# A matmul behind a sigmoid on one core: h made twice by ScalarE, and other shares of t for GpSimd

## The chip, the core and the metric

The kernel runs on one core of one Trainium2 chip. The time is the device time of one execution, in microseconds (us). Before the change three executions took 314.30, 316.69 and 318.40 us, median 316.69. A further execution was recorded by the hardware profiler; all rows here come from it.

Engines are called by their short names: PE (TensorE), DVE (VectorE), ACT (ScalarE), Pool (GpSimd), and SP (SyncE), which issues nearly all transfers. PEld is PE's loading of weights.

## The reference

```python
# x (1024, 24, 1024), W1 (1024, 24), b1 (1024), W2 (1024, 1024), b2 (1024), all fp32
h = jax.nn.sigmoid(jnp.einsum('bts,st->bs', x, W1) + b1)
return h @ W2.T + b2
```

x is 100.7 MB. For each row b and column s the 24 values over t are weighted and summed, b1 is added, the sigmoid gives h (1024 x 1024), and one product with W2 follows.

## The kernel before

**Stages.** There are four stages, each 512 rows of x by 512 columns s: stage 0 is rows 0 to 511, columns 0 to 511; stage 1 the same rows, the other columns; stages 2 and 3 are the other rows. One t of a stage is one ring load, [128, 4, 512] fp32, 1.05 MB (four row tiles of 128). A stage has 24 t.

**Two ways for a t.** The first t of a stage (4 in stage 0, 6 in the others: third number of its row in `STAGES`) go to Pool. They are loaded as halves of two row tiles into `nat` (6 slots, 0.52 MB each); Pool multiplies each half by its weights (`weigh`, L589) and adds it to the running sum of its half (`add_sum`, L598). The other t are loaded into `ring` (5 slots). PE transposes each (`turn_unit`, L303) into one of 6 PSUM banks `xbank`: a unit is one column block c of 128 columns (c = 0 to 3) with its 2 or 4 row tiles. DVE multiplies the unit by the weight, which now is one value a partition, and adds it to `acc` (`add_unit`, L423; the first unit of a stage and c is written by L417). Pool's sum of a stage is transposed in the same way, once, as four "n" units (DVE L421); before the change they stand ahead of the units of t = 22.

**Parts.** In stages 2 and 3 the last t (6 and 10) are loaded and summed in two parts: first row tiles 0 and 1 of all of them, then row tiles 2 and 3 of all of them. A ring slot then holds two half loads. The rows of part 1 are finished early and their products can run while part 2 is read.

**h and the products.** When a column block's sum is done, ACT makes h from it (L535) and rounds it to `h_hi` (fp32r, L539). DVE makes `h_lo` = h - h_hi (`low_part`, L437; in the last stage's last rows DVE does the rounding too, L472 and L474). W2 is transposed and split in the same way during stage 0 (L332, L498, L430). An output tile [128, 512] is 4 column blocks times three products, h_hi w_hi, h_hi w_lo and h_lo w_hi (L375). The product steps of stage i are dealt out between the units of stage i+1 by `steps_due` and the table `STRETCHES`. Sums of stages 0 and 2 are kept in `y` by ACT (`keep_out`, L523), those of stages 1 and 3 are added to it by DVE (`add_out`, L453) and stored. In the last stage 36 steps of part 1's rows lie between the units of part 2, 12 (`REST`) behind the last unit, and then the 48 products of the last rows follow (L401).

**Order of the loads.** SP issues in one fixed order: the ring loads of a stage one after the other, and ahead of those whose index is in the stage's tuple `places` a `nat` load of this or the next stage. Each waits for its slot:

```python
if m >= NATS and parts[m - NATS][1] < pools[parts[m - NATS][0]] - 1:
    sp.wait_ge(nat_added, sums_made(m - NATS + 2))
elif m >= NATS:
    sp.wait_ge(unit_turned, sum_turned(parts[m - NATS][0], parts[m - NATS][2]))
```

The second branch (L263's wait) is for a slot that held a stage's finished sum: it is free when PE has turned the n units of its rows. A ring load (L269) waits until the last unit of the load five slots back is turned. Whatever SP waits for, the loads behind it wait too.

Of the kernel before, what the change touches and what calls it, by code (L numbers as in the profile page):

```python
# [32 lines left out]
def rec_kernel(nc, x, W1, b1, W2, b2, out):  # L33
# [94 lines left out]
    with ExitStack() as ctx:  # L128
# [156 lines left out]
        def _(pe):  # L285
# [196 lines left out]
        def _(act):  # L482
            act.dma_start(b1row[:, :], b1.rearrange("(c p) -> c p", p=P)).then_inc(b1_loaded, 16)
            for p in (0, 32):
                act.dma_start(h[p:p + 1, 0:OH, :], b2.rearrange("(a h n) -> a h n", a=1, n=BANK)).then_inc(b2_loaded, 16)
# [44 lines left out]
            def sigmoid(i, p):  # L530

                c, row, n = sums[i][p]
                rows = slice(row * P, (row + n) * P)
# [1 line left out]
                nc.scalar.activation(h[:, c, rows], acc[:, c, rows], ACT.Sigmoid,  # L535
                                     bias=b1col[:, bass.ds(STAGES[i][1] + c, 1)]).then_inc(h_ready, 1)
# [88 lines left out]
```

## Time and profile before

| what | us |
|---|---|
| median of three executions | 316.69 |
| profiled execution | 314.37 |
| its span on the core | 312.5 |
| DVE busy | 268.9 |
| PE busy | 265.0 |
| Pool busy | 196.6 |
| ACT busy | 53.6 |
| mean granted clock of PE | 0.95 |

Busy time of an engine is no bound by itself: PE and DVE feed each other through `xbank`, and both wait for loads. GB/s over time says where transfers are the pace, the queue's own waits say what held SP, and the chain of work that ended last says what ran at the end. The duration of one matmul in the rows overlaps the next, so rates are taken from a run of them (time over count). The same holds for DVE.

### The profile page before, as it was taken

How to read it: one execution, taken by the hardware profiler on the slowest of the kernel's cores; microseconds unless marked ns; L12 is line 12 of the kernel's file. 1: busy time of each engine (PE TensorE's matmuls, PEld its weight loads, DVE VectorE, ACT ScalarE, POOL GpSimd, SP SyncE). 2: the span in 40 equal slices, each digit the busy share in tenths (PEclk: the TensorE clock that was granted, in tenths of full speed). 3: DMA queues.
4: the chain of work that ended last, by engine and by line, in shares of the span. 5: the costliest groups of instructions: out<-in, count | busy, mean ns of one | idle time of the engine just before them, and what ended most of it. 6: DMA issues, size and time to landing. Idle time of an engine off the chain costs nothing.

```text
span 312.5 us, 4880 instructions
## 1 busy us (share of the span) xinstructions
PE 265.0 (85%) x1761; PEld 227.6 (73%) x1761; DVE 268.9 (86%) x452; ACT 53.6 (17%) x97; POOL 196.6 (63%) x89
## 2 busy tenths in 40 slices
PE   0948788857887799999968699997699999999995
PEld 0847688747865588888756588886488888788884
DVE  0719997929989998888999999999999999899961
ACT  4201222302262011011140000004032001050200
POOL 3119766635379888985679996967979399700000
PEclk9968977979999999999989999999579999999999
DMA  7999999999999999999999999999979999992122
GB/s 218 393 388 387 387 385 387 402 386 387 386 387 386 387 386 387 386 386 387 385 386 387 386 393 389 396 385 388 381 265 343 398 387 387 387 387 111 68 103 101
DMA packets 55164, 109.48 MB, mean 350 GB/s; under 512 B 3418, under 2 KB 3426, under 8 KB 55140
## 3 DMA queue, kind: packets, MB, share of 16 engines
q1 hardware_dynamic: 54544, 107.06, 93.3%
q10 hardware_dynamic: 596, 2.11, 1.7%
q8 instruction: 14, 0.23, 0.3%
q14 instruction: 10, 0.08, 0.1%
HBM read 104.97 MB, written 4.19 MB: 349 GB/s over the span
## 4 chain that ended last, share of the span: by engine, by line
PE 53%; DMA 17%; issue 13%; DVE 9%; ACT 3%; SPq 3%; DVEq 0%; ACTq 0%
PE xbank L303 27%; PE pbank L375 19%; DMA ring<-in_r_x 17%; DVE acc L423 7%; PE xbank L401 3%; SPq L263 2%; ACT h L535 2%; PE pbank L321 2%; ACT h_hi L539 1%; PE pbank L365 1%; PE pbank L332 1%; DVE acc L421 1%; DVE y L453 1%; DVE w_lo L430 1%; SPq L269 1%
## 5 line engine op out<-in xcount | busy, mean ns | idle before, releaser
L423 DVE SCALAR_TENSOR_TENSOR acc<-xbank,w,acc 128x512 f32<-128x512 f32 (+1 forms) x344 | 203.5, 643 | 22.8 <-PE xbank L303 21.4
L303 PE MATMUL xbank<-ident,ring 128*128 128x128 f32 x1184 | 186.4, 285 | 39.1 <-DMA ring<-in_r_x 27.5
L303 PEld LDWEIGHTS xbank<-ident,ring 128*128 128x128 f32 x1184 | 151.3, 147 | 70.9 <-DVE acc L423 24.4
L589 POOL TENSOR_TENSOR nat<-nat,w1all 128x1024 f32<-128x1024 f32 x44 | 106.1, 2413 | 67.3 <-DMA nat<-in_r_x 53.5
L598 POOL TENSOR_TENSOR nat<-nat 128x1024 f32<-128x1024 f32 x36 | 87.1, 2420 | 2.8
L375 PE MATMUL pbank<-w_hi,h_hi 128*128 128x512 f32 x112 | 52.9, 472 | 1.8 <-DVE y L453 1.8
L375 PE MATMUL pbank<-w_lo,h_hi 128*128 128x512 f32 x112 | 51.6, 461 | 0.0
L375 PE MATMUL pbank<-w_hi,h_lo 128*128 128x512 f32 x112 | 45.8, 453 | 0.0
L535 ACT ACTIVATE h<-acc,b1col 128x256 f32<-128x256 f32 (+2 forms) x28 | 14.5, 536 | 93.3 <-DVE acc L423 93.2
L437 DVE TENSOR_TENSOR h_lo<-h,h_hi 128x256 fp32r<-128x256 f32 (+1 forms) x20 | 26.3, 1314 | 0.0
L375 PEld LDWEIGHTS pbank<-w_hi,h_hi 128*128 128x128 f32 x112 | 22.0, 197 | 2.2 <-DVE y L453 2.0
L523 ACT COPY y<-pbank 128x512 f32<-128x512 f32 x16 | 9.4, 587 | 81.1 <-PE pbank L375 81.1
L375 PEld LDWEIGHTS pbank<-w_lo,h_hi 128*128 128x128 f32 x112 | 22.2, 198 | 0.2
L417 DVE TENSOR_SCALAR acc<-xbank,w 128x512 f32<-128x512 f32 x16 | 11.8, 748 | 11.7 <-PE xbank L303 9.3
L375 PEld LDWEIGHTS pbank<-w_hi,h_lo 128*128 128x128 f32 x112 | 19.5, 190 | 0.2
L498 ACT CAST w_hi<-pbank 128x512 fp32r<-128x512 f32 x16 | 9.4, 587 | 39.5 <-PE pbank L332 39.5
L332 PE MATMUL pbank<-ident,y 128*128 128x128 f32 x64 | 10.5, 289 | 0.9 <-DVE w_lo L430 0.9
L303 PE MATMUL xbank<-ident,nat 128*128 128x128 f32 x64 | 10.6, 291 | 0.5 <-DVE acc L423 0.5
L421 DVE TENSOR_TENSOR acc<-xbank,acc 128x256 f32<-128x256 f32 (+1 forms) x24 | 10.9, 501 | 0.0
L430 DVE TENSOR_TENSOR w_lo<-pbank,w_hi 128x512 fp32r<-128x512 f32 x16 | 10.9, 680 | 0.0
L493 ACT COPY w1all<-pbank 128x512 f32<-128x512 f32 x12 | 7.0, 587 | 18.1 <-PE pbank L321 18.1
L539 ACT CAST h_hi<-h 128x256 fp32r<-128x256 f32 (+1 forms) x20 | 9.8, 491 | 0.6
(31 smaller groups left out, 93.9 us busy)
## 6 DMA issues: line engine op xcount, KB each, us to landing
ring<-in_r_x SPq DMA_DIRECT2D x58, 1024.0 KB, 12.9
nat<-in_r_x SPq DMA_DIRECT2D x44, 512.0 KB, 12.8
ring<-in_r_x SPq DMA_DIRECT2D x32, 512.0 KB, 11.5
y<-in_L_rec_W SPq DMA_DIRECT2D x2, 2048.0 KB, 15.3
out_y<-y ACTq DMA_DIRECT2D x4, 512.0 KB, 7.3
out_y<-y SPq DMA_DIRECT2D x8, 256.0 KB, 2.0
w<-in_L_rec_W SPq DMA_DIRECT2D x1, 96.0 KB, 2.5
h<-in_L_rec_b ACTq DMA_DIRECT2D x2, 4.0 KB
```

What stands on the lines that cost most here:

```text
L303: mm = pe.transpose(xbank[u % XBANKS][:, a * P:(a + 1) * P], tile, ident[:, :])
L332: mm = pe.transpose(pbank[m % 2][:, j * P:(j + 1) * P], y[:, j, c * P:(c + 1) * P], ident[:, :])
L375: mm = pe.matmul(pbank[n % 2][:, :], a[:, c, rows], w[:, STAGES[i][1] + c, cols], start=r == 0, stop=r == per - 1)
L417: nc.vector.tensor_scalar(total, bank, weight, None, ALU.mult).then_inc(unit_added, 1)
L421: nc.vector.tensor_tensor(total, bank, total, ALU.add).then_inc(unit_added, 1)
L423: nc.vector.scalar_tensor_tensor(out=total, in0=bank, scalar=weight, in1=total, op0=ALU.mult, op1=ALU.add).then_inc(unit_added, 1)
L430: nc.vector.tensor_tensor(w_lo[:, c, cols], pbank[m % 2][:, :], w_hi[:, c, cols].bitcast(F32), ALU.subtract).then_inc(w_lo_ready, 1)
L437: nc.vector.tensor_tensor(h_lo[:, c, rows], h[:, c, rows], h_hi[:, c, rows].bitcast(F32), ALU.subtract).then_inc(h_lo_ready, 1)
L535: nc.scalar.activation(h[:, c, rows], acc[:, c, rows], ACT.Sigmoid, bias=b1col[:, bass.ds(STAGES[i][1] + c, 1)]).then_inc(h_ready, 1)
L539: nc.scalar.copy(h_hi[:, c, rows], h[:, c, rows]).then_inc(h_hi_ready, 1)
L589: nc.gpsimd.tensor_tensor(slot, slot, row, ALU.mult).then_inc(nat_weighed, 1)
L598: nc.gpsimd.tensor_tensor(slot, slot, nat[:, (m - 2) % NATS, :, :], ALU.add).then_inc(nat_added, 1)
```

## The change

ACT makes h twice for every piece: first the sigmoid rounded straight into `h_hi`, then the same sigmoid in fp32 into one PSUM bank, `hbank`, from which DVE subtracts `h_hi` to make `h_lo`. `h` in SBUF is gone. Since there is one bank, the second sigmoid waits until the low part before it is made. The bank comes from `xbank` (6 to 5). The low parts move forward in DVE's order: of a whole stage, they stand behind the first four units of the next one. In the last rows ACT rounds too, not DVE.

Pool gets 7 t in stages 1 to 3 (6 before), `nat` 7 slots; the table of places changes with it. The last stage has 8 t in two parts (10 before). The n units of a stage or part move from ahead of t = 22 to behind t = 23. The row of b2 uses the last `nat` slot before its first load, which waits for `b2_ready`.

```diff
-    (4, 0, 6, 6, (0, 2, 3, 5, 6, 8, 9, 11, 12, 14, 18, 20, 21, 23), "keep"),
-    (4, 4, 6, 10, (1, 3, 4, 6, 7, 9, 11, 13), "last"),
+    (4, 0, 7, 6, (0, 1, 3, 4, 5, 7, 8, 9, 10, 12, 14, 17, 19, 21), "keep"),
+    (4, 4, 7, 8, (0, 1, 2, 4, 5, 6, 8, 9, 11, 13), "last"),
...
-    NATS = 6
-    XBANKS = 6
+    NATS = 7
+    XBANKS = 5
...
         for t, row, n in loads[i]:
-            if t == T - 2:
+            order += [("x", t, c, row, n) for c in range(NC)]
+            if t == T - 1:
                 order += [("n", 0, c, row, n) for c in range(NC)]
-            order += [("x", t, c, row, n) for c in range(NC)]
...
-        h = sb("h", [P, NC, BANK])
...
+        hbank = ctx.enter_context(nc.psum_tensor("hbank", [P, BANK], F32))
...
+        def h_held(i, p):
+
+            return hbank[:, :sums[i][p][2] * P]
...
+                        if m == NATS - 1:
+
+                            sp.wait_ge(b2_ready, 1)
...
             def low_part(i, p):
+
                 c, row, n = sums[i][p]
                 rows = slice(row * P, (row + n) * P)
-                dve.wait_ge(h_hi_ready, first_sum[i] + p + 1)
-                nc.vector.tensor_tensor(h_lo[:, c, rows], h[:, c, rows], h_hi[:, c, rows].bitcast(F32),
+                dve.wait_ge(h_ready, first_sum[i] + p + 1)
+                nc.vector.tensor_tensor(h_lo[:, c, rows], h_held(i, p), h_hi[:, c, rows].bitcast(F32),
                                         ALU.subtract).then_inc(h_lo_ready, 1)
...
-                if splits[i]:
-                    lows.update({part_end(i) + NC + 2 * c: (i, c) for c in range(NC)})
-                if i < LAST:
-                    lows.update({first_unit[i + 1] + NC + 2 * c: (i, len(sums[i]) - NC + c) for c in range(NC)})
+                for p in range(len(sums[i]) if i < LAST else TAIL):
+                    c, row, _ = sums[i][p]
+                    if splits[i] and row == 0:
+                        u = part_end(i) + 1 + 2 * c
+                    else:
+                        u = first_unit[i + 1] + c
+                    lows.setdefault(u, []).append((i, p))
...
-                nc.vector.tensor_copy(h_hi[:, c, rows], h[:, c, rows]).then_inc(tail_hi, 1)
-                dve.wait_ge(tail_hi, p - TAIL + 1)
-                nc.vector.tensor_tensor(h_lo[:, c, rows], h[:, c, rows], h_hi[:, c, rows].bitcast(F32),
+                nc.vector.tensor_tensor(h_lo[:, c, rows], h_held(LAST, p), h_hi[:, c, rows].bitcast(F32),
                                         ALU.subtract).then_inc(tail_lo, 1)
...
                 act.wait_ge(unit_added, sum_end(i, p))
-                nc.scalar.activation(h[:, c, rows], acc[:, c, rows], ACT.Sigmoid,
-                                     bias=b1col[:, bass.ds(STAGES[i][1] + c, 1)]).then_inc(h_ready, 1)
-                if i < LAST or p < TAIL:
-                    act.wait_ge(h_ready, first_sum[i] + p + 1)
-                    nc.scalar.copy(h_hi[:, c, rows], h[:, c, rows]).then_inc(h_hi_ready, 1)
+                tail = i == LAST and p >= TAIL
+                nc.scalar.activation(h_hi[:, c, rows], acc[:, c, rows], ACT.Sigmoid,
+                                     bias=bias).then_inc(tail_hi if tail else h_hi_ready, 1)
+
+                g = first_sum[i] + p
+                if tail and p > TAIL:
+                    act.wait_ge(tail_lo, p - TAIL)
+                elif g > 0:
+                    act.wait_ge(h_lo_ready, g)
+                nc.scalar.activation(h_held(i, p), acc[:, c, rows], ACT.Sigmoid, bias=bias).then_inc(h_ready, 1)
```

SP's order at the passage from stage 0 to stage 1. `nat` waits either for Pool's additions (nat_added) or for PE's transposes (unit_turned). Before:

```order
L263 DMA nat<-in_r_x 128x2x512 [waits nat_added]
L269 DMA ring<-in_r_x 128x4x512 [waits unit_turned] x2
L263 DMA nat<-in_r_x 128x2x512 [waits nat_added]
L269 DMA ring<-in_r_x 128x4x512 [waits unit_turned] x2
L263 DMA nat<-in_r_x 128x2x512 [waits nat_added]
L269 DMA ring<-in_r_x 128x4x512 [waits unit_turned]
L263 DMA nat<-in_r_x 128x2x512 [waits unit_turned]
```

Before, the first pair of ring loads here is the last of stage 0 (t = 22 and 23), and three ring loads of stage 1 stand ahead of the `nat` load that waits for unit_turned. After:

```order
L271 DMA nat<-in_r_x 128x2x512 [waits nat_added]
L277 DMA ring<-in_r_x 128x4x512 [waits unit_turned] x2
L271 DMA nat<-in_r_x 128x2x512 [waits nat_added]
L277 DMA ring<-in_r_x 128x4x512 [waits unit_turned]
L271 DMA nat<-in_r_x 128x2x512 [waits unit_turned]
```

After it, the first pair is again t = 22 and 23 of stage 0; one ring load of stage 1 stands ahead of the `nat` load that waits for unit_turned.

PE's order at the end of stage 0, where `xbank<-ident,nat` are the n units, `pbank<-ident,y` the transposes of W2, and `xbank<-ident,ring` the x units. Before:

```order
L303 MATMUL xbank<-ident,nat 128x128 x8
L332 MATMUL pbank<-ident,y 128x128 x4
L303 MATMUL xbank<-ident,nat 128x128 x8
L303 MATMUL xbank<-ident,ring 128x128 x4
L332 MATMUL pbank<-ident,y 128x128 x4
L303 MATMUL xbank<-ident,ring 128x128 x12
L332 MATMUL pbank<-ident,y 128x128 x4
L303 MATMUL xbank<-ident,ring 128x128 x52
```

After:

```order
L340 MATMUL pbank<-ident,y 128x128 x4
L311 MATMUL xbank<-ident,ring 128x128 x12
L340 MATMUL pbank<-ident,y 128x128 x4
L311 MATMUL xbank<-ident,nat 128x128 x16
L311 MATMUL xbank<-ident,ring 128x128 x36
```

The 16 transposes of the n units have moved behind all x units of the stage.

DVE's order at the start of stage 1, behind the last sum of stage 0. Before:

```order
L417 TENSOR_SCALAR acc<-xbank,w 128x512 [waits h_ready,unit_turned] x4
L423 SCALAR_TENSOR_TENSOR acc<-xbank,w,acc 128x512 [waits unit_added,unit_turned]
L437 TENSOR_TENSOR h_lo<-h,h_hi 128x512 [waits h_hi_ready]
L423 SCALAR_TENSOR_TENSOR acc<-xbank,w,acc 128x512 [waits unit_added,unit_turned] x2
L437 TENSOR_TENSOR h_lo<-h,h_hi 128x512 [waits h_hi_ready]
```

After:

```order
L426 TENSOR_SCALAR acc<-xbank,w 128x512 [waits h_ready,unit_turned]
L447 TENSOR_TENSOR h_lo<-hbank,h_hi 128x512 [waits h_ready]
L426 TENSOR_SCALAR acc<-xbank,w 128x512 [waits h_ready,unit_turned]
L447 TENSOR_TENSOR h_lo<-hbank,h_hi 128x512 [waits h_ready]
L426 TENSOR_SCALAR acc<-xbank,w 128x512 [waits h_ready,unit_turned]
```

Each low part now stands directly behind the first unit of its column block, and both wait for the second sigmoid.

## Rows read from the trace of the kernel before

**Rows 1.** The page, parts 1 and 2: busy us by engine; GB/s in 40 slices.
```profile
PE 265.0 (85%) x1761; PEld 227.6 (73%) x1761; DVE 268.9 (86%) x452; ACT 53.6 (17%) x97; POOL 196.6 (63%) x89
...
GB/s 218 393 388 387 387 385 387 402 386 387 386 387 386 387 386 387 386 386 387 385 386 387 386 393 389 396 385 388 381 265 343 398 387 387 387 387 111 68 103 101
```

**Rows 2.** The page, parts 3 and 6: bytes; a DMA issue with its size and us to landing.
```profile
HBM read 104.97 MB, written 4.19 MB: 349 GB/s over the span
...
out_y<-y SPq DMA_DIRECT2D x8, 256.0 KB, 2.0
```

**Rows 3.** SP's own waits by line: us in total, times, longest.
```profile
SPq L263 <- PE xbank L303: 24.9, 6, 11.1
```

**Rows 4.** SP's timeline from 212 us: start us, us, engine line operation.
```profile
214.64 2.49 SPq L269 DMA_DIRECT2D ring<-in_r_x  x2
...
228.23 0.37 SPq L263 DMA_DIRECT2D nat<-in_r_x  x1
```

**Rows 5.** Windows, stage 2 to 3: busy us by engine, PE clock, DMA share, GB/s.
```profile
core 0: us, PE busy (x) PEld busy (x) DVE busy (x) ACT busy (x) POOL busy (x), PEclk, DMA share, GB/s
...
221.00:223.00 2.00, 1.78 (x6) 1.28 (x6) 2.00 (x3) 0.00 (x0) 1.99 (x1) 0.50 1.05 388
...
225.00:227.00 2.00, 1.47 (x8) 0.86 (x6) 2.00 (x5) 0.00 (x0) 2.00 (x2) 0.50 0.91 339
...
227.00:229.00 2.00, 2.00 (x9) 1.64 (x8) 2.00 (x6) 0.00 (x0) 1.92 (x2) 0.50 0.23 89
...
229.00:231.00 2.00, 2.00 (x13) 1.64 (x12) 1.55 (x5) 0.00 (x0) 1.44 (x1) 0.76 0.79 209
...
235.00:237.00 2.00, 2.00 (x16) 1.76 (x15) 1.85 (x4) 0.95 (x2) 2.00 (x1) 1.00 0.83 247
...
237.00:239.00 2.00, 2.00 (x17) 1.76 (x15) 2.00 (x4) 0.59 (x1) 2.00 (x2) 1.00 0.91 306
```

**Rows 6.** Groups by line and shape: count, busy us, mean ns, idle before and releaser.
```profile
L535 ACT ACTIVATE h<-acc,b1col 128x512 f32<-128x512 f32 x8 | 5.8, 719 | 8.4 <-DVE acc L423 8.4
...
L437 DVE TENSOR_TENSOR h_lo<-h,h_hi 128x512 fp32r<-128x512 f32 x8 | 13.3, 1665 | 0.0
...
L437 DVE TENSOR_TENSOR h_lo<-h,h_hi 128x256 fp32r<-128x256 f32 x12 | 13.0, 1079 | 0.0
...
L430 DVE TENSOR_TENSOR w_lo<-pbank,w_hi 128x512 fp32r<-128x512 f32 x16 | 10.9, 680 | 0.0
...
L589 POOL TENSOR_TENSOR nat<-nat,w1all 128x1024 f32<-128x1024 f32 x44 | 106.1, 2413 | 67.3 <-DMA nat<-in_r_x 53.5 <-ACT w1all L493 13.8
...
L598 POOL TENSOR_TENSOR nat<-nat 128x1024 f32<-128x1024 f32 x36 | 87.1, 2420 | 2.8
```

**Rows 7.** Timeline of PE at the start of stage 1: start us, us, [idle, releaser].
```profile
88.03 2.30 PE L303 MATMUL xbank<-ident,ring 128*128 128x128 f32 x16 [0.50 <-DMA ring<-in_r_x]
```

**Rows 8.** Timeline of DVE: a run of full units; a low part with Pool quiet.
```profile
106.07 11.30 DVE L423 SCALAR_TENSOR_TENSOR acc<-xbank,w,acc 128x512 f32<-128x512 f32 x17
...
278.26 0.41 DVE L437 TENSOR_TENSOR h_lo<-h,h_hi 128x256 fp32r<-128x256 f32 x1
```

**Rows 9.** Timeline of Pool and of ACT: one load awaited, the first sum of part 1.
```profile
215.63 2.35 POOL L589 TENSOR_TENSOR nat<-nat,w1all 128x1024 f32<-128x1024 f32 x1 [0.32 <-DMA nat<-in_r_x]
...
275.30 0.51 ACT L535 ACTIVATE h<-acc,b1col 128x256 f32<-128x256 f32 x1 [1.81 <-DVE acc L423]
```

**Rows 10.** The chain that ended last: start us, us, engine, tile, line, count.
```profile
146.07 3.07 PE xbank L303 x28
...
266.38 0.63 PE xbank L303 x4
...
295.50 2.99 PE pbank L375 x13
...
298.50 10.89 PE xbank L401 x48
...
309.41 0.69 DVE y L453
```

More of the change, by code:

```diff
@@ L21 @@
 STAGES = (
-    (0, 0, 4, 0, (2, 3, 5, 7, 9, 11, 13, 15, 17, 18), "keep"),
-    (0, 4, 6, 0, (0, 2, 3, 5, 6, 8, 9, 11, 12, 14, 15, 17), "last"),
-    (4, 0, 6, 6, (0, 2, 3, 5, 6, 8, 9, 11, 12, 14, 18, 20, 21, 23), "keep"),
-    (4, 4, 6, 10, (1, 3, 4, 6, 7, 9, 11, 13), "last"),
+    (0, 0, 4, 0, (2, 3, 5, 7, 9, 11, 12, 13, 15, 16, 17, 18), "keep"),
+    (0, 4, 7, 0, (0, 1, 3, 4, 5, 7, 8, 9, 11, 12, 13, 14, 15, 16), "last"),
+    (4, 0, 7, 6, (0, 1, 3, 4, 5, 7, 8, 9, 10, 12, 14, 17, 19, 21), "keep"),
+    (4, 4, 7, 8, (0, 1, 2, 4, 5, 6, 8, 9, 11, 13), "last"),
 )
-CUT = 2
 NC = 4
@@ L41, in rec_kernel @@
     RING = 5
-    NATS = 6
-    XBANKS = 6
+    NATS = 7
+    XBANKS = 5
     REST = 12
+    CUT = JT // 2
     assert (B, T, S, O) == (2 * BANK, 24, 1024, 1024)
@@ L348, in product_step @@
                     n, r = (k - 2 * high) // NC, high + (k - 2 * high) % NC
-                first = n == 0
                 n += OH * row
@@ L368, in product_step @@
                     c, a, w = (r - bias) // 2, h_hi, (w_hi, w_lo)[(r - bias) % 2]
-                    if first:
+                    if n % (OH * CUT) == 0:
                         pe.wait_ge(h_hi_ready, first_sum[i] + sum_of(i, c, j) + 1)
@@ L372, in product_step @@
                     c, a, w = r - high, h_lo, w_hi
-                    if first:
+                    if n % (OH * CUT) == 0:
                         pe.wait_ge(h_lo_ready, first_sum[i] + sum_of(i, c, j) + 1)
@@ L398, in _ @@
                     if n % OH == 0:
-                        pe.wait_ge(tail_lo, sum_of(LAST, c, j) - TAIL + 1)
+                        pe.wait_ge(tail_hi, sum_of(LAST, c, j) - TAIL + 1)
                     for k, (a, w) in enumerate(((h_hi, w_hi), (h_hi, w_lo), (h_lo, w_hi))):
+                        if n % OH == 0 and k == 2:
+                            pe.wait_ge(tail_lo, sum_of(LAST, c, j) - TAIL + 1)
                         mm = pe.matmul(bank[:, :], a[:, c, j * P:(j + 1) * P], w[:, STAGES[LAST][1] + c, cols],
@@ L461, in _ @@
                         split_w2(W2S[v - 2])
-                    if u in lows:
-                        low_part(*lows[u])
+                    for piece in lows.get(u, ()):
+                        low_part(*piece)
                     for g in range(outs_due(u - 2), outs_due(u - 1)):
@@ L484, in _ @@
             for p in (0, 32):
-                act.dma_start(h[p:p + 1, 0:OH, :], b2.rearrange("(a h n) -> a h n", a=1, n=BANK)).then_inc(b2_loaded, 16)
+                act.dma_start(nat[p:p + 1, NATS - 1, :, :], b2.rearrange("(a h n) -> a h n", a=1, n=BANK)).then_inc(b2_loaded, 16)
             def keep_set(q):
@@ L504, in _ @@
                 nc.scalar.copy(b2x[p:p + 1, :].rearrange("a (h n) -> a h n", n=BANK),
-                               h[p:p + 1, 0:OH, :]).then_inc(b2_rounded, 1)
+                               nat[p:p + 1, NATS - 1, :, :]).then_inc(b2_rounded, 1)
             for q in range(EARLY):
@@ L533, in sigmoid @@
                 rows = slice(row * P, (row + n) * P)
+                bias = b1col[:, bass.ds(STAGES[i][1] + c, 1)]
                 act.wait_ge(unit_added, sum_end(i, p))
[L535 to L539 removed]
+                tail = i == LAST and p >= TAIL
[7 more added lines that the diff above has]
+                nc.scalar.activation(h_held(i, p), acc[:, c, rows], ACT.Sigmoid, bias=bias).then_inc(h_ready, 1)
             act.wait_ge(set_kept, 1)
@@ L559, in _ @@
                     if i > 0:
-                        act.wait_ge(h_lo_ready, min(first_sum[i], first_sum[LAST]))
                         act.wait_ge(out_summed, OUTS * (i - 1) + OH * (row + n))
@@ L576, in _ @@
             low = b2x[32:33, :].rearrange("a (h n) -> a h n", n=BANK)
-            nc.gpsimd.tensor_tensor(low, h[32:33, 0:OH, :], low.bitcast(F32), ALU.subtract).then_inc(b2_ready, 1)
+            nc.gpsimd.tensor_tensor(low, nat[32:33, NATS - 1, :, :], low.bitcast(F32), ALU.subtract).then_inc(b2_ready, 1)
             pool.wait_ge(b2_ready, 1)
```

## The prediction

> **What bounds the kernel now.** I read the page first. DVE is busy 268.9 us and PE 265.0 us of 312.5, and the transfers run at 386 to 388 GB/s in nearly every slice from the second to the 35th, with one dip, to 265 and 343, in slices 30 and 31 [rows 1]. 104.97 MB are read [rows 2]; at 0.387 MB a microsecond that is 271 us. So transfers set the pace up to about 284 us, and busy engines there mostly keep up. What remains is the dip and what follows the last load.
>
> The dip comes from SP's own waits: one of 11.1 us at L263, a load into `nat`, for PE's transposes [rows 3]. It ends at 228.23, and SP had issued nothing since about 217 [rows 4]. The slot wanted is the one that held the last sum of stage 2, which is free only when the "n" units are turned. The windows give the price. Against 387 GB/s the three windows from 225 to 231 lack 48, 298 and 178 GB/s over 2 us each: 524 x 2 / 387 = 2.7 us [rows 5]. From 235 to 239 another 140 and 81 are lacking, 1.1 us, of which about 0.6 us comes back in faster slices behind. I take 3.2 us for all of it. The queue was dry by 225 + (339 + 89) x 2 / 387 = 227.2 and the flow came back, as if at once, 2.7 us later, at 229.9: 1.7 us after SP's issue.
>
> The end: the chain is PE from 266.38, when it last waits for a load, to 309.41 [rows 10]. That load is the sixth of part 1 of the last stage, and 14 more half loads of 0.524 MB (1.354 us each) come behind it, so the last lands at 266.4 + 14 x 1.354 = 285.2, and PE ends 24.2 us later. Costs: a transposed tile 3.07 / 28 = 0.11 us, a product 10.89 / 48 = 0.227 us [rows 10]. Part 2 has 88 tiles (10 t x 4 x 2, and 8 of sums) and 8 + 36 + 12 + 48 = 104 products: 9.8 + 23.6 = 33.4 us, back from 309.4 to 276.0; ACT meets the first finished sum of part 1 at 275.30 [rows 9], which agrees. PE is the bound there. Behind PE's end come 3.1 us of addition and store.
>
> **The change, part by part.** (1) *The low part from PSUM.* The subtraction at L437 takes 1.67 us for 512 columns (8 of them) and 1.08 for 256 (12) while Pool works, but 0.41 for 256 once Pool is silent [rows 6, 8]; the same operation with one operand in PSUM takes 0.68 for 512 at any time (L430) [rows 6]. DVE saves 8 x 1.0 + 12 x 0.67 = 16 us. (2) *Seven t.* Three stages drop one t each, 12 units of DVE at 11.30 / 17 = 0.66 us [rows 8], 8 us, and 12 x 4 x 0.11 = 5 us of PE; Pool gets 12 more operations of 2.41 us [rows 6], 29 us, and is at 226 us. Per stage Pool needs 26 x 2.41 = 63 us where transfers take 25.17 MB / 0.387 = 65. Following its queue load by load I find it at most about 2 us behind a landing, and its last sum ready near 273, before part 2 wants it. Pool's cost is 0, with 3 us as the upper bound if it slips.
>
> All this is taken off engines that are not the bound before 266 us. DVE's relief removes the backlog behind the old dip: at stages 2 to 3 SP is then not late. This gives back the 3.2 us.
>
> (3) *The sums turn last.* The "n" units move from before the last two t to behind the last one, and the load that needs their slot moves forward: in the order SP has it as the second `nat` load of stages 1 and 2, with only one `nat` and one ring load between it and the previous stage. Once the last ring load of a stage lands (time L), the queue holds 1.354 + 2.71 = 4.06 us of work. A load counts as landed some time after its bytes are moved: a store of 256 KB takes 2.0 us, of which 0.7 is bytes, so 1.3 for start and end together [rows 2]; I take 1.2 us and dry at L + 2.8. As an upper bound: the `nat` load landed at 215.63 [rows 9] has 14.9 us of transfers behind it up to the dip, which makes 230.5 against the 227.2 found, a lag of 3.3 us, so the queue may be dry 2.1 us earlier. When is SP released? At stage 0 to 1, PE turns 4 x units, two W2 sets and 4 n units, 40 tiles x 0.11 = 4.4 us (DVE, with 5 banks, needs L + 0.5 + 3 x 0.66 + 0.5, which is less). Issue at L + 4.5, flow at L + 6.2: a hole of 3.4 us. L is here 86.7: the first ring load of stage 1 landed at 88.0 before [rows 7], stage 0's last 4.06 earlier, and two more `nat` loads, 2.7 us, now go ahead of it. At stage 1 to 2 it is 32 tiles, 3.5 us: flow at L + 5.3, a hole of 2.5 us. Before, three ring and two `nat` loads of the new stage went ahead of that wait and the sums turned 8 units earlier, and no dip is seen there [rows 1]. At stage 2 to 3 the wait is behind two `nat` and two ring loads, 8.1 us: dry at L + 6.9, and the half-size units are turned by L + 2.9, flow at L + 4.7. No hole, with 2.2 us to spare.
> The bounds of the two holes together: 1.5 us (restart in 0.5 us and no lag) to 10 (a lag of 3.3 in both).
> Of the restart the Trainium skill ("DMA: Bandwidth & Descriptors", Specifications) says about 0.6 us to the first byte from SyncE's path. The rows show 1.7 to full flow; with 0.6 both holes would lose 1.1 us, an estimate of 2.2 less in the sum. The measured row decides.
>
> (4) *ACT makes h twice.* In the first units of a stage each column piece is now a chain: second sigmoid 0.72 [rows 6], DVE's first product into `acc` 0.66, the low part 0.68, hand-overs, and only then the next second sigmoid, since one bank holds h: 2.2 us x 4 = 8.8 us, where before only the sigmoid and the rounding copy went from piece to piece. Transfers run on meanwhile: five ring slots hold 5 x 3.8 us. PE does 4 tiles and two products per unit in 4 x 0.11 + 2 x 0.227 = 0.9 us, 3.6 to 3.7 a load, where a load with its share of `nat` takes (17 x 2.71 + 14 x 1.354) / 17 = 3.83, so the backlog is carried but doesn't grow. Cost 0; with the cover gone, some 3 to 5 us a stage. At the end the same chain (two sigmoids or a sigmoid and a low part a piece, under 0.8 us) starts before PE is through its 12 remaining products, 2.7 us, and PE wants the fourth piece 2 us later still: 0. The copy that DVE did there is gone, off the path.
>
> (5) *Eight t in two parts.* Part 2 has 72 tiles and still 104 products: 7.9 + 23.6 = 31.5 us, 1.8 less. But it starts later against the last landing: part 1's last load lands 8 x 1.354 = 10.8 us before it, not 13.5. Following PE over the half loads of part 1 (8 tiles and 3 products, 1.57 us, against 1.354, with `nat` loads between that let it catch up, then the sums, 1.57) PE ends part 1 about 7.0 us before the last landing, where it was 9.2. So PE's end is last landing + 24.5 to 24.7 in place of 24.2: +0.4 us. Bounds -0.5 and +1.
>
> **Sum.** The profiled execution took 314.37 us, a span of 312.5 and 1.9 around it. -3.2 (old dip) + 3.4 + 2.5 (new holes) + 0.4 (end) = +3.1: 317.5 us, 1.0% slower in its own terms. The median shown is 316.69, 2.3 above the profiled run, and the three runs spread over 4 us. The same ratio on the median gives 319.8; I place the forecast between the two, at 319.
>
> **The rivals.**
> *A, no holes.* Landing and restart overlap better than I think, or PE turns its sums sooner. For it: in stages 0 to 2 of before no slice dips. Against: nothing there waits for sums just turned; where it did, 2.7 us were lost. Then -3.2 + 0.4 = -2.8: 311.6 in its own terms, 312.5 to 313.9 as a median.
> *B, the third boundary drains too.* The place is the third `nat` load of the last stage. It decides where PE is more than 2.2 us later than reckoned at the end of stage 2. Before, PE was several us behind there, its clock at 0.50 and DVE never idle from 221 to 229 [rows 5], with the slow low parts in it. If that returned, by the chain of (4) or by Pool still holding DVE, the hole would be about 5 us and the dips of the first two places would grow by 1: +9, 323.6, as a median 325. Against it: the low part loses its slow form.
> TensorE's clock could feed this. The rows show it at 1.2 GHz (0.50) from 221 to 229, with PE partly idle in front [rows 5]. The Trainium skill ("TensorE: Matmul & The Clock Gate", What's actually happening) has the throttled state as the default that activity releases; by that the long chain at a stage's start puts PE at half speed there, an estimate of up to 5 us of backlog, of which the ring covers all but the last. It stands inside rival B.
> *C, the change doesn't do what it says*: the subtraction from PSUM still takes its long form. Then DVE keeps 16 us more; transfers still bound, result near B.
>
> **How the numbers follow.** Forecast 0.58, A 0.20, B and C 0.18, anything else 0.04. A reaches down to 312; B's middle is 325, so the range is 312 to 325. About 2% is what a measurement of this kernel can tell from no change: 310.4 to 323.0. Faster by over 2%: only if A goes with a shorter end too, 0.05. Slower by over 2%: B, C and the upper part of the lag bound, 0.18. Within 2%: 0.77.
>
> **What would show it.** Right: two new dips in GB/s, near 90 and 155 us, each behind an SP wait at the `nat` load; no dip near 228; low parts at 0.6 and 0.4 us; last landing 2 to 4 us later than 285, PE ending 24 to 25 us behind it. Wrong: flat 387 GB/s across 85 to 165 us (A), a dip near 230 with PE's clock at 0.50 (B), or Pool's sums awaited by PE at a stage's end, which I have at nothing.

## The result, and the profile after

The changed kernel took 321.08 us (median of four runs, 319.03 to 321.76) where before took 315.5 on the same chip: ratio 1.019, 95% interval 1.010 to 1.028. It is slower, by about 6 us; whether by more or less than 2% stays unclear. The profiled execution took 321.65 us (span 319.9) where the one of before took 314.37: +7.3 us.

The page, parts 1 and 2, of the changed kernel (busy us by engine; GB/s in 40 slices of 8.0 us), to be held against [rows 1]:

```profile
PE 258.4 (81%) x1721; PEld 221.4 (69%) x1721; DVE 248.2 (78%) x424; ACT 58.6 (18%) x107; POOL 221.6 (69%) x101
...
GB/s 219 399 388 387 387 387 386 401 387 385 386 161 392 386 387 386 387 384 386 328 213 389 388 392 391 395 387 387 387 367 364 395 388 387 388 387 112 66 56 142
```

DVE has 21 us less to do and PE 7 us less, and the kernel is slower. The GB/s line says why: slice 12 (88 to 96 us) falls to 161, slices 20 and 21 (152 to 168 us) to 328 and 213, and the old dip in slices 30 and 31 is now shallow. At the `nat` loads, SP's waits for PE have grown from the 24.9 us of [rows 3]; those for Pool have not. The changed kernel's two lines, then the one for Pool of before:

```profile
SPq L271 <- PE xbank L311: 37.8, 6, 12.9
SPq L271 <- POOL nat L614: 8.5, 6, 4.7
```
```profile
SPq L263 <- POOL nat L598: 11.3, 7, 3.4
```

SP's timeline shows how, at each of the three passages from stage to stage, a `nat` load that waits for PE's transposes goes out 9 to 14 us after the load before it (start us, us, engine line operation); [rows 4] has the third place of before:

```profile
78.12 1.23 SPq L277 DMA_DIRECT2D ring<-in_r_x  x1
91.71 0.37 SPq L271 DMA_DIRECT2D nat<-in_r_x  x1
...
147.64 1.31 SPq L277 DMA_DIRECT2D ring<-in_r_x  x1
161.91 0.37 SPq L271 DMA_DIRECT2D nat<-in_r_x  x1
...
224.17 1.24 SPq L277 DMA_DIRECT2D ring<-in_r_x  x1
233.64 0.37 SPq L271 DMA_DIRECT2D nat<-in_r_x  x1
```

The windows around them, with the columns of [rows 5] (the last three: PE clock, DMA share, GB/s):

```profile
88.00:90.00 2.00, 2.00 (x21) 2.00 (x20) 2.00 (x4) 0.64 (x2) 1.60 (x1) 1.00 0.38 144
90.00:92.00 2.00, 1.68 (x16) 1.40 (x13) 2.00 (x4) 0.54 (x1) 1.92 (x2) 1.00 0.01 5
92.00:94.00 2.00, 1.72 (x12) 1.25 (x12) 2.00 (x5) 1.08 (x1) 1.21 (x1) 1.00 0.56 100
...
158.00:160.00 2.00, 2.00 (x12) 2.00 (x11) 1.75 (x3) 0.00 (x0) 2.00 (x2) 0.50 0.38 137
160.00:162.00 2.00, 2.00 (x18) 2.00 (x17) 1.90 (x4) 0.61 (x1) 1.92 (x2) 0.89 0.00 0
162.00:164.00 2.00, 1.62 (x15) 1.39 (x13) 2.00 (x4) 1.34 (x3) 2.00 (x1) 1.00 0.52 81
...
234.00:236.00 2.00, 2.00 (x15) 1.67 (x14) 1.52 (x4) 1.21 (x4) 1.92 (x2) 1.00 0.96 290
...
242.00:244.00 2.00, 2.00 (x15) 1.74 (x14) 2.00 (x5) 0.00 (x0) 1.92 (x2) 1.00 0.95 286
```

Read as the prediction reads them, with the queue counted as dry from the moment at which all bytes would have been moved at full speed: the first hole lasts from 88 + 144 x 2 / 387 = 88.7 to 94 - 105 x 2 / 387 = 93.5, 4.7 us. The second lasts from 158.7 to 163.6, 4.9 us. The third place lacks 0.5 us at 234 and 0.5 at 242. Over the whole read, windows below 387 less those above it, 9.3 us of transfer time are lost; the same count gives 2.6 us for before. The end of the reads, counted in the same way, moves from 283.5 to 290.2 us (last windows with reads: 282 + (268 + 30) x 2 / 387, and 288 + (349 + 74) x 2 / 387). These 6.7 us are nearly the whole difference. The rest is the end. The chain, with the columns of [rows 10]:

```profile
305.82 10.89 PE xbank L410 x48
316.74 0.69 DVE y L466
```

PE ends 26.5 us behind the end of the reads, before 25.9: +0.7 us. The trace also has the time from a load's issue to its landing. By it the last load lands at 285.8 us before and at 292.0 in the changed kernel, and PE ends 23.6 and 24.7 us behind it: 6.2 + 1.1 is the same 7.3 us, parted otherwise. The first sum of part 1 meets ACT at 284.32 us, 5.9 us ahead of the end of the reads; [rows 9] has 275.30, 8.2 ahead.

Narrow windows around the first hole show that neither edge is sharp:

```profile
88.40:88.80 0.40, 0.40 (x6) 0.40 (x5) 0.40 (x1) 0.39 (x1) 0.40 (x1) 1.00 0.50 189
89.20:89.60 0.40, 0.40 (x6) 0.40 (x5) 0.40 (x2) 0.00 (x0) 0.40 (x1) 1.00 0.20 77
90.40:90.80 0.40, 0.40 (x6) 0.40 (x5) 0.40 (x1) 0.14 (x1) 0.38 (x1) 1.00 0.00 0
...
92.50:92.70 0.20, 0.20 (x4) 0.19 (x2) 0.20 (x1) 0.00 (x0) 0.20 (x1) 1.00 0.00 0
92.70:92.90 0.20, 0.20 (x4) 0.03 (x1) 0.20 (x2) 0.00 (x0) 0.20 (x1) 1.00 1.32 143
```

The flow thins out from about 88 to 90.4 us, and the last load in the queue (SP's row at 78.12) lands at 90.88, within 0.5 us of the last bytes. So 88.7 is no moment at which anything happens; it only gives the hole its area.

The groups that answer to [rows 6] (count, busy us, mean ns):

```profile
L605 POOL TENSOR_TENSOR nat<-nat,w1all 128x1024 f32<-128x1024 f32 x50 | 118.7, 2376 | 53.0 <-DMA nat<-in_r_x 40.1 <-ACT w1all L504 12.9
...
L447 DVE TENSOR_TENSOR h_lo<-hbank,h_hi 128x512 fp32r<-128x512 f32 x8 | 5.5, 682 | 0.0
...
L447 DVE TENSOR_TENSOR h_lo<-hbank,h_hi 128x256 fp32r<-128x256 f32 x12 | 5.0, 417 | 0.0
```

The low parts take 0.68 and 0.42 us where they took 1.67 and 1.08, so the change does what it says. The Trainium skill ("SBUF — State Buffer", Who interferes with whom) has VectorE and GpSimd compete for one pair of SBUF ports, with an exclusive lock; the two durations agree with it, since an operand in PSUM leaves the pair alone, and so do the 0.41 us of [rows 8] with both operands in SBUF and Pool quiet. Pool's operations cost the same as before.

The chain at the start of a stage, DVE's timeline (in brackets the idle time before, and what ended it):

```profile
97.80 0.75 DVE L426 TENSOR_SCALAR acc<-xbank,w 128x512 f32<-128x512 f32 x1 [0.83 <-ACT hbank L556]
98.47 0.68 DVE L447 TENSOR_TENSOR h_lo<-hbank,h_hi 128x512 fp32r<-128x512 f32 x1
99.98 0.75 DVE L426 TENSOR_SCALAR acc<-xbank,w 128x512 f32<-128x512 f32 x1 [0.83 <-ACT hbank L556]
```

One piece every 2.18 us, 2.2 in the prediction.

### The profile page after: what moved, and what is told of

It reads as the page before. It is cut to its first block, busy times and chain, and to the rows that moved or that the text cites. A ratio compares the mean times of both kernels' runs of the same rounds, so it can differ in the third digit from the quotient of the medians.

```text
span 319.9 us, 4777 instructions
## 1 busy us (share of the span) xinstructions
PE 258.4 (81%) x1721; PEld 221.4 (69%) x1721; DVE 248.2 (78%) x424; ACT 58.6 (18%) x107; POOL 221.6 (69%) x101
## 4 chain that ended last, share of the span: by engine, by line
DMA 41%; PE 41%; DVE 7%; SPq 4%; issue 4%; ACT 2%; ACTq 0%; DVEq 0%
DMA ring<-in_r_x 41%; PE xbank L311 20%; PE pbank L382 15%; PE xbank L410 3%; SPq L271 3%; DVE acc L432 3%; DVE acc L426 2%; ACT hbank L556 1%; DVE h_lo L447 1%; PE pbank L372 1%; SPq L277 1%; DVE w_lo L439 1%; DVE acc L430 1%; DVE y L466 0%; ACT L548 0%
## 5 line engine op out<-in xcount | busy, mean ns | idle before, releaser
L432 DVE SCALAR_TENSOR_TENSOR acc<-xbank,w,acc 128x512 f32<-128x512 f32 (+1 forms) x324 | 198.3, 655 | 44.3 <-PE xbank L311 39.5
L311 PE MATMUL xbank<-ident,ring 128*128 128x128 f32 x1136 | 179.3, 286 | 55.5 <-DMA ring<-in_r_x 46.7
L311 PEld LDWEIGHTS xbank<-ident,ring 128*128 128x128 f32 x1136 | 145.0, 148 | 87.5 <-DVE acc L432 28.6
L605 POOL TENSOR_TENSOR nat<-nat,w1all 128x1024 f32<-128x1024 f32 x50 | 118.7, 2376 | 53.0 <-DMA nat<-in_r_x 40.1
L614 POOL TENSOR_TENSOR nat<-nat 128x1024 f32<-128x1024 f32 x42 | 99.8, 2377 | 3.3
L382 PE MATMUL pbank<-w_hi,h_hi 128*128 128x512 f32 x112 | 50.7, 453 | 0.0
L548 ACT ACTIVATE h_hi<-acc,b1col 128x256 fp32r<-128x256 f32 (+2 forms) x28 | 14.8, 528 | 83.9 <-DVE acc L430 83.9
L556 ACT ACTIVATE hbank<-acc,b1col 128x256 f32<-128x256 f32 (+2 forms) x28 | 14.1, 505 | 11.5 <-DVE h_lo L447 10.8
L504 ACT COPY w1all<-pbank 128x512 f32<-128x512 f32 x14 | 8.2, 587 | 26.5 <-PE pbank L329 26.5
L329 PE MATMUL pbank<-ident,w 128*128 128x128 f32 x56 | 9.3, 292 | 1.6 <-DVE w_lo L439 1.6
L447 DVE TENSOR_TENSOR h_lo<-hbank,h_hi 128x256 fp32r<-128x256 f32 (+1 forms) x20 | 10.5, 523 | 0.0
```

The source lines that it names most:

```text
L311: mm = pe.transpose(xbank[u % XBANKS][:, a * P:(a + 1) * P], tile, ident[:, :])
L382: mm = pe.matmul(pbank[n % 2][:, :], a[:, c, rows], w[:, STAGES[i][1] + c, cols], start=r == 0, stop=r == per - 1)
L432: nc.vector.scalar_tensor_tensor(out=total, in0=bank, scalar=weight, in1=total, op0=ALU.mult, op1=ALU.add).then_inc(unit_added, 1)
L447: nc.vector.tensor_tensor(h_lo[:, c, rows], h_held(i, p), h_hi[:, c, rows].bitcast(F32), ALU.subtract).then_inc(h_lo_ready, 1)
L548: nc.scalar.activation(h_hi[:, c, rows], acc[:, c, rows], ACT.Sigmoid, bias=bias).then_inc(tail_hi if tail else h_hi_ready, 1)
L556: nc.scalar.activation(h_held(i, p), acc[:, c, rows], ACT.Sigmoid, bias=bias).then_inc(h_ready, 1)
```

## The experiments

The experiments ran in three sessions (E1 to E4; E5 to E8; E9 to E11), each on one chip and with its own runs of before, whose medians were 315.52, 314.11 and 314.45 us. Each ratio is against the runs of before in its session, with its 95% interval, and kernels of different sessions are compared by ratio. Before has the same median in the first session as in the result above, so there the times are held against the changed kernel's 321.08 directly.

**E1: only the sums turned early again.** The changed kernel, with the n units ahead of t = 22 as before:

```diff
-            order += [("x", t, c, row, n) for c in range(NC)]
-            if t == T - 1:
+            if t == T - 2:
                 order += [("n", 0, c, row, n) for c in range(NC)]
+            order += [("x", t, c, row, n) for c in range(NC)]
```

> The kernel after with one edit: the n units go back to ahead of t = 22. Theory W (SP's nat load waits for sums that are turned last, and the loads behind it wait too): SP is released 8 units earlier, the dips near 90 and 160 us (4.6 and 4.8 us of transfers lost) and the small one near 235 (0.9) mostly go, median 311 to 313 where the kernel after has 321.1. Rival Q (the long chain of two sigmoids and a low part per column block at a stage's start, or Pool's larger share, costs the time): chain and share are unchanged, so it stays at 319 or more, with the dips still there.

Measured: 313.55 us (313.21 to 313.86), ratio 0.996 (0.993 to 0.999). That is 7.5 us under the changed kernel. The page's GB/s line and SP's waits:

```profile
GB/s 208 404 387 388 386 387 386 401 388 386 386 387 385 386 387 386 387 386 387 366 389 387 387 390 391 396 386 387 386 387 404 386 387 387 386 355 22 67 57 147
```
```profile
SPq L271 <- PE xbank L311: 22.4, 6, 7.6
```

Only 0.4 us is lacking in slice 20 (366), and slices above 387 give back more; no hole is left, the third place included. Everything else of the change is still in, the new places of the `nat` loads, the chain of part (4) and the single bank too. So without the late sums there are no holes, and the chain alone makes none.

**E2: only the place of the waiting load.** The sums stay last, and the `nat` loads of stages 1 and 2 move back behind three ring loads:

```diff
-    (0, 4, 7, 0, (0, 1, 3, 4, 5, 7, 8, 9, 11, 12, 13, 14, 15, 16), "last"),
-    (4, 0, 7, 6, (0, 1, 3, 4, 5, 7, 8, 9, 10, 12, 14, 17, 19, 21), "keep"),
+    (0, 4, 7, 0, (0, 3, 4, 5, 6, 7, 8, 9, 11, 12, 13, 14, 15, 16), "last"),
+    (4, 0, 7, 6, (0, 3, 4, 5, 6, 7, 8, 9, 10, 12, 14, 17, 19, 21), "keep"),
```

> The kernel after with one edit: the second nat load of stages 1 and 2 moves from index 1 to index 3, and the following ones from 3, 4, 5, 7 to 4, 5, 6, 7, so three ring loads go ahead of the wait; n units stay last. Theory W: 9.5 us of transfers are queued in place of 4.1, so the first two dips go although PE turns its sums as late as now: median 312 to 314, the small dip near 235 stays. Rival Q: 319 or more. A third possibility: Pool gets seven halves in a row at 4.06 us each and needs 4.8, SP then waits for nat_added and a new dip of 1 to 3 us comes, median 314 to 317.

Measured: 314.14 us (313.67 to 314.94), ratio 0.997 (0.994 to 1.000), 6.9 us under the changed kernel. SP's waits by line:

```profile
SPq L271 <- PE xbank L311: 26.8, 5, 9.4
```

The first hole is gone and the second shrinks to 1.0 us. The third place, whose own order is untouched, loses 1.6 us at 226 to 230 and 0.7 at 234. Net 2.3 us are lost. With E1 this shows that both halves are needed for the first two holes: a sum turned late, and a load close behind the boundary that waits for it. The third possibility, SP waiting for Pool, did not cost what was feared: SP's longest wait for Pool, 5.0 us, falls between 234 and 239, where at most the 0.7 us are lost.

**E3: PE kept busy ahead of the second boundary.** The product steps of stage 0 are spread to 8 units before the end of stage 1 instead of four fifths of it:

```diff
-            (OUTS * steps_of(0), first_unit[1] + 2 * NC, first_unit[1] + len(units[1]) * 4 // 5),
+            (OUTS * steps_of(0), first_unit[1] + 2 * NC, first_unit[1] + len(units[1]) - 2 * NC),
```

> The kernel after with one edit: the product steps of stage 0 are spread to 8 units before the end of stage 1, not over its first four fifths, so PE is busy up to the last load. Theory C (the second hole is 4.8 us and not 2.5 because PE, partly idle from 148 on, turns the last units at the 0.50 clock): granted clock 1.00 from 156 to 160 us, SP released 1.5 to 2 us earlier after the last landing, median 319 to 319.5. Rival L (the hole is larger because loads land later behind their bytes): clock or not, the hole stays at 4.5 to 5 us and the median at 321.

Measured: 319.72 us (319.34 to 320.70), ratio 1.015 (1.009 to 1.021), 1.4 us under the changed kernel. First PE's timeline of the changed kernel ahead of its second hole, then that of E3:

```profile
152.46 1.94 PE L311 MATMUL xbank<-ident,ring 128*128 128x128 f32 x16 [1.66 <-DMA ring<-in_r_x]
156.52 3.19 PE L311 MATMUL xbank<-ident,ring 128*128 128x128 f32 x16 [2.13 <-DMA ring<-in_r_x]
159.51 2.36 PE L311 MATMUL xbank<-ident,nat 128*128 128x128 f32 x16
```
```profile
156.60 1.94 PE L311 MATMUL xbank<-ident,ring 128*128 128x128 f32 x16 [0.49 <-DMA ring<-in_r_x]
158.37 1.91 PE L311 MATMUL xbank<-ident,nat 128*128 128x128 f32 x16
```

The windows of E3:

```profile
158.00:160.00 2.00, 2.00 (x20) 2.00 (x19) 2.00 (x5) 0.00 (x0) 2.00 (x2) 1.00 0.34 124
160.00:162.00 2.00, 1.74 (x16) 1.51 (x15) 2.00 (x4) 1.32 (x3) 1.92 (x2) 1.00 0.35 43
162.00:164.00 2.00, 0.49 (x5) 0.25 (x3) 1.63 (x3) 0.96 (x2) 2.00 (x1) 1.00 0.94 340
```

In the changed kernel PE has run out of products and waits for loads twice, 1.66 and 2.13 us. At 158 to 160 its granted clock is 0.50, the lower of the two levels, and 32 tiles take 161.9 - 156.5 = 5.4 us. In E3 PE has products between the tiles, the clock stays at 1.00, and the 32 tiles take 3.7 us. SP is released at 160.31, not 161.91, and the hole is 3.4 us instead of 4.9. The last ring load of the stage lands at the same time in both, 156.4 and 156.5 us, and the queue is dry at 158.7 and 158.6, so nothing of the difference comes from the loads (rival L). The Trainium skill ("TensorE: Matmul & The Clock Gate", What's actually happening) has the slow state as the default; the rows agree.

**E4, E9: only the two sigmoids.** The kernel before with `hbank`, 5 `xbank`, the new low parts and their places, and the waits that belong to them; six t for Pool, the n units, `places` and ten t in two parts as before. Its core:

```diff
-    XBANKS = 6
+    XBANKS = 5
...
-                dve.wait_ge(h_hi_ready, first_sum[i] + p + 1)
-                nc.vector.tensor_tensor(h_lo[:, c, rows], h[:, c, rows], h_hi[:, c, rows].bitcast(F32),
+                dve.wait_ge(h_ready, first_sum[i] + p + 1)
+                nc.vector.tensor_tensor(h_lo[:, c, rows], h_held(i, p), h_hi[:, c, rows].bitcast(F32),
```

> The kernel before with the h part of the change alone: two sigmoids, one PSUM bank, 5 xbanks, low parts at their new places; 6 t for Pool, 10 t in two parts and early n units as before. Theory W: the low parts fall from 1.67 and 1.08 us to 0.68 and 0.41, DVE's backlog at the end of stage 2 is smaller and the old dip near 228 (3.2 us) shrinks to 0 to 2: median 312 to 315 where before has 315.5. Rival Q: the chain of 2.2 us per column block at each stage's start delays the loads: 317 or more.

Measured: 313.57 us (312.28 to 314.46), ratio 0.994 (0.991 to 0.997). The dip at 228 is gone, but 1.7 us are lost at 172 to 176 (1.2 in E9, the same kernel again, and 0.7 in E8), which E1, E2, E3 and E10, with seven t for Pool, do not show. Its windows, PE's timeline ahead of them, and SP's waits at the ring loads:

```profile
166.00:168.00 2.00, 0.75 (x4) 0.75 (x5) 1.55 (x3) 0.34 (x1) 1.50 (x1) 0.51 1.05 386
168.00:170.00 2.00, 2.00 (x9) 1.70 (x8) 2.00 (x4) 0.00 (x0) 1.23 (x1) 0.50 1.06 389
170.00:172.00 2.00, 2.00 (x8) 1.61 (x7) 1.92 (x4) 0.00 (x0) 1.92 (x2) 0.50 1.04 383
172.00:174.00 2.00, 2.00 (x13) 1.68 (x12) 1.29 (x3) 0.00 (x0) 2.00 (x2) 0.79 0.60 226
```
```profile
165.07 0.66 PE L308 MATMUL xbank<-ident,ring 128*128 128x128 f32 x4 [1.52 <-DVE acc L424]
167.25 1.12 PE L308 MATMUL xbank<-ident,ring 128*128 128x128 f32 x4 [1.52 <-DVE acc L424]
```
```profile
SPq L274 <- PE xbank L308: 138.9, 67, 7.1
```

The chain lets PE turn four tiles every 2.18 us and leaves it idle for 1.52 of them. Then the clock falls to 0.50 for some 6 us, just where products are dealt out, and a ring load waits 7.1 us. But E10 has the same chain and the same 6 us at 0.50 there, and loses nothing (385 and 388 GB/s from 172 to 176). So chain and clock alone don't make this dip; it comes with six t for Pool and their order of loads, and which of these makes the difference was not tried.

**E5, E7, E8: how many t in two parts.** E5 is E1 with 10 t, E7 is E1 with 12 (and other `places` in the last stage), E8 is E4 with 8. E5's edit, in the last row of `STAGES`:

```diff
-    (4, 4, 7, 8, (0, 1, 2, 4, 5, 6, 8, 9, 11, 13), "last"),
+    (4, 4, 7, 10, (0, 1, 2, 4, 5, 6, 8, 9, 11, 13), "last"),
```

> The kernel after with the n units back ahead of t = 22, and 10 t in two parts instead of 8 (7 t for Pool). Theory P (eight t in two parts cost about 0.45 us a pair against ten, because PE's part 2 starts 2.7 us later for 1.8 us less of work): PE ends 0.4 to 1 us closer to the end of the transfers than with 8, median 312.5 to 313.2 where the same with 8 had 313.55. Rival: the parts don't matter, or the longer run of half loads lets PE fall behind: 313.5 to 315.

> As the run before with 12 t in two parts, Pool's places at every second half load. Theory P: another 0.4 us off at most, 312 to 313. Rival: Pool's last loads come too late with half loads between them and PE waits for its sum ahead of t = 22: 314 to 317.

> The kernel before with the h part of the change, and 8 t in two parts instead of 10 (6 t for Pool, early n units): the split alone, against 313.57 with 10. Theory P: 0.4 to 1 us slower, 314 to 314.6, PE's end 0.5 us further behind the end of the transfers. Rival: no difference or faster, 313.6 or less.

Measured: E5 312.89 us, ratio 0.995 (0.992 to 0.998); E7 313.01, 0.995 (0.992 to 0.998); E8 313.86, 0.998 (0.995 to 1.001), just under what was expected. Ten and twelve can't be told apart. E8 lies 0.4% above E4 by ratio, in the direction of part (5), but the intervals overlap.

**E6: only the late sums, in the kernel before.**

```diff
-            if t == T - 2:
-                order += [("n", 0, c, row, n) for c in range(NC)]
             order += [("x", t, c, row, n) for c in range(NC)]
+            if t == T - 1:
+                order += [("n", 0, c, row, n) for c in range(NC)]
```

> The kernel before with one edit: the n units last. Theory W says that late sums cost only where too few ring loads are queued ahead of the wait: three ring and two nat loads (10.8 us) stand ahead of it at the first two places, so no hole there; at the third, where one more unit group is awaited while PE is behind, the old dip of 3.2 us grows by 2 to 4: median 317 to 320. Rival (late sums alone make the first two holes): dips near 90 and 155 us here too, 321 or more.

Measured: 321.17 us (318.70 to 322.33), ratio 1.019 (1.013 to 1.026). That is above what was expected and where the rival put it, so the windows must decide between them. SP's timeline, the windows, and one of DVE's low parts:

```profile
217.09 2.65 SPq L269 DMA_DIRECT2D ring<-in_r_x  x2
235.90 0.37 SPq L263 DMA_DIRECT2D nat<-in_r_x  x1
```
```profile
228.00:230.00 2.00, 1.11 (x5) 0.60 (x5) 2.00 (x5) 0.00 (x0) 1.92 (x2) 0.50 0.44 162
230.00:232.00 2.00, 2.00 (x9) 1.64 (x9) 2.00 (x7) 0.00 (x0) 1.07 (x1) 0.50 0.03 12
232.00:234.00 2.00, 2.00 (x10) 1.64 (x10) 1.39 (x4) 0.00 (x0) 0.00 (x0) 0.57 0.00 0
234.00:236.00 2.00, 2.00 (x16) 1.71 (x15) 1.94 (x6) 0.78 (x2) 0.00 (x0) 1.00 0.00 0
236.00:238.00 2.00, 2.00 (x16) 1.75 (x15) 1.83 (x4) 1.94 (x6) 0.00 (x0) 1.00 0.46 86
```
```profile
226.70 2.15 DVE L437 TENSOR_TENSOR h_lo<-h,h_hi 128x256 fp32r<-128x256 f32 x1
```

With the places of before the first boundary stays at 383 to 391 GB/s and the second loses 1.4 us; the rival's two holes aren't there. The third loses 8.7 us: the sums turn last behind the slow low parts of before (1.79 to 2.15 us each here) and PE at half clock. This is the mechanism of rival B, at more than its price. In the changed kernel, with fast low parts and PE's clock at 1.00 from 220 on, the third place loses near 1 us; it also has seven t, other places and other parts there, so that the fast low parts alone keep the hole small is argued, not shown.

**E9, E10, E11: the three best in one session.** E9 is the kernel of E4, E10 of E5, E11 of E1.

> The kernel of e4_h_only once more, now beside e10 and e11 on one chip, to rank the three. Theory 1 (holes are all that matters, and the rest of the versions differ only in the end): e4 lost 1.1 us of transfers and its PE ended 25.9 us behind them, e5 and e1 lost none but ended 28 us behind; the sums are within 1 us of each other, so this one 0.993 to 0.997 of before. Theory 2 (the seventh t for Pool is worth something of its own): this one is the slowest of the three by 1 us or more.

> The kernel of e5_early_split10 once more (seven t for Pool, ten t in two parts, sums turned ahead of t = 22). If part (5) of the prediction has the sign right, this one is 0.3 to 1 us below e11, which differs by eight t in two parts alone. If eight and ten cost the same, within 0.2 us. Against before 0.994 to 0.996.

> The kernel of e1_n_early once more (eight t in two parts). Against before 0.995 to 0.998; 0.3 to 1 us above e10 by part (5) of the prediction, no difference if the share in two parts costs nothing.

Measured: E9 313.26 us (312.78 to 314.09), ratio 0.997 (0.994 to 0.999); E10 313.02 (312.65 to 313.91), 0.993 (0.990 to 0.996); E11 313.39 (312.81 to 313.90), 0.996 (0.993 to 1.000). All three lie under before, by 0.3 to 0.7%, which is near the edge of what the intervals can tell. E10 has the lowest median, by 0.24 and 0.37 us, less than the ranges. E10 and E11 differ in the parts alone, and the 0.37 us are in the direction and at the lower edge of what was expected; their ratios lie further apart, 0.3%. So 15 us less on DVE (busy 254.3 us in E4), and 21 us less with Pool's seventh t in E10 and E11, are worth 1 to 2 us where transfers set the pace.

## Why the prediction was right, point by point

The sign and the mechanism were right, and the median of 321.08 lies within 312 to 325. In the prediction's own terms it said +3.1 us and the profiled runs differ by 7.3; both holes were priced too low. That the median is still only 2.1 us above the forecast of 319 is in part luck: the forecast stood on a median of before of 316.69, which came out as 315.5 with a fourth run. Against before it said +2.3 us on the medians, and the measured difference is 5.6. The last landing moved by 6.2 us, for the 2 to 4 I had given as a sign of being right. The range reached as high as it did for the sake of rival B, which didn't happen as described.

- **Old dip, -3.2.** The dip at 228 is gone in E4 and nearly so in the changed kernel, where about 1 us is lost at 234 and 242 in its place. The term was about 1 us too large: the step "at stages 2 to 3 SP is then not late" had 2.2 us to spare, with SP due at L + 2.9. The last ring load of stage 2 lands at 228.8 and SP comes at 233.64, L + 4.8: 1.9 of the 2.2 us were gone.
- **First hole, 3.4; measured 4.7.** The last ring load of stage 0 goes out at 72.89 and takes 14.1 us to land, so L = 87.0, for 86.7:

```profile
DMA to landing us min/median/max: 14.1/14.1/14.1
```

SP came at 91.71, L + 4.7 for L + 4.5, and flow was back 93.5 - 91.7 = 1.8 us later, for 1.7. But the queue counts as dry at 88.7, L + 1.8, not L + 2.8. The failed step is the time from bytes moved to landing: of the 4.06 us of work behind the load only 1.8 were left when it landed, so landing was 2.3 us late on the bytes in this count, and I had taken 1.2 from a store's 2.0 us. My upper bound, 3.3, contained it. The reason shows in the narrow windows: the flow thins out over some 2 us, and the last load in the queue lands 2.1 us after 88.7 but within 0.5 us of its own last bytes.
- **Second hole, 2.5; measured 4.9.** The last ring load of stage 1 lands at 156.4 (PE's wait for it ends at 156.5). Dry at L + 2.3, 0.5 us earlier than assumed, and SP released at L + 5.5 instead of L + 3.6. E3 shows the cause of that second part: at full clock SP comes at L + 3.8 and the hole is 3.4 us. I had let the clock into rival B alone, behind the chain at a stage's start, and had not asked what PE does in the last fifth of stage 1, where `STRETCHES` deals it no products.
- **Restart.** Counted to full flow, the two holes show 1.8 and 1.7 us, for the 1.7 of the prediction. The Trainium skill ("DMA: Bandwidth & Descriptors", Specifications) gives about 0.6 us to the first byte. The trace agrees, counted from the end of SP's row: that row is 91.71 + 0.37 = 92.08, and in windows of 0.2 us the first bytes show at 92.70; in E3 the row ends at 160.68 and they show at 161.3. But full flow comes later still, and a hole is priced by full flow; with 0.6 the forecast would have been lower and worse.
- **Low parts, seven t.** As predicted: 0.68 and 0.42 us, Pool at 221.6 us (226 said), DVE -20.7 us (-24 said). Pool's operations cost nothing in E1, E5 and E7, whose reads net lose none.
- **The chain, cost 0.** Right for this kernel: the period is 2.18 us, and behind it PE's clock does fall to 0.50 (from 168 to 174 us, with 386 to 392 GB/s), as rival B's sentence on the clock has it, but nothing is lost there. The "0.9 us a unit" of PE holds at full clock only, and the ring covered it. In E4, with six t, 1.7 us are lost in that place.
- **The end, +0.4; measured +0.7** against the end of the reads and +1.1 against the last landing, just above my bound of 1. PE ends 24.7 us behind the last landing, as forecast (24.5 to 24.7); it was before that ended 23.6 and not 24.2 us behind it, since its last load landed at 285.8 and not 285.2. The parts alone, with early sums, are worth what I said: 24.2 us in E1 and E11 with eight t, 23.8 in E5 and E10 with ten. Part 1's first sum came 2.3 us later against the end of the reads, where I had reckoned 2.2.
- **Rivals.** A (no holes) was refuted. B's place lost 1 us in the changed kernel and 8.7 in E6. C was refuted by the low parts. (B's +9 on 314.37 gives 323.4, not 323.6; nothing hangs on it.)

The sum with measured terms: 4.7 + 4.9 + 1.0 = 10.6 us lost in dips, less the 2.7 + 1.1 of before, is 6.8, for the 6.7 us by which the reads end later (what faster slices give back is 1.2 to 1.3 us in both); with 0.7 for the end, 7.4, for the 7.3 measured.

A warning on the end of the reads as a mark: in E1, counted as if at full speed, they end at 280.3 us and PE ends 28.2 us later, where before and E4 have 25.9. That looks like a loss at the end, and is none. The last reads of E1 trickle on at 20 to 41 GB/s until 284, the last load lands at 284.3, and PE ends 24.2 us behind that, against 24.7 in the changed kernel, 23.6 in before and 23.5 in E4.

It stays open why E4 dips at 172 and what the rest of the +1.1 us at the end is beyond the parts. Nor was it tried whether a second bank for h, which would break the chain, gains anything.

## What to carry to other kernels

Before a table of load places is shifted, ask of each load in an in-order queue what its slot waits for, and count the work already queued between that wait and the last event that can release it: here two loads, 4.06 us, of which only about 2 us were left once the last load had landed. Relief on engines that aren't the pace is worth little (1 to 2 us here), and moving one wait forward by three loads together with a later release cost more than all of it (holes of 4.7 and 4.9 us), though neither of the two alone made these holes. Look too at what a pausing engine does to its own clock: here the tiles at a boundary took 5.4 us behind a stretch in which PE idled and 3.7 us behind one in which it had products.

## What the runs showed of the hardware that was not expected

- A queue that nobody fills doesn't run dry at once: in the changed kernel the flow thinned from about 88 to 90.4 us (189, 77, then 0 GB/s in the narrow windows), and at the second hole from 158 to 160. The last load landed at 90.9 and 160.3, within 0.5 us of the last bytes. Counted as area, the queue was dry 1.8 and 2.3 us after the stage's last load had landed, with 4.06 us of loads behind it.
- A hole opened by an empty queue costs 1.7 to 1.8 us beyond the moment at which the next load is issued: 1.8 and 1.7 in the changed kernel, 1.7 in E3 and in before. The first bytes come 1.0 us after the issue (92.7 after 91.71, 161.3 after 160.31 in E3).
- PE's granted clock fell to 0.50 after a stretch in which it was busy for a third of the time (0.66 to 0.75 of 2 us in E4) and stayed there for some 6 us, though from 168 us on PE was busy throughout.
- Sixteen transposes took 1.94 us at clock 1.00; those started at 156.52, with the clock at 1.00 in the first microsecond and 0.51 in the second, took 3.19 us.
